# Odd experts' results copied by VectorE instead of ScalarE, in both experts' stages

## The reference, cut to what matters

```
x = x + 0.5 * ffn(layernorm(x));  x = x + attn(layernorm(x));  x = x + 0.5 * ffn(layernorm(x))

def ffn(h):                       # 64 experts, 2 per token, at most 256 rows each
    x = rmsnorm(h) * rms_w
    probs = softmax(x @ gate_w.T);  topk_w, topk_ids = top_k(probs, 2), weights normalised
    xb = rows of x sorted into 64 experts x 256 slots
    g, u = split(xb @ w13)        # 256 -> 2 x 128, for each expert
    yb = (silu(g) * u) @ w2       # 128 -> 256, for each expert
    out = sum over the 2 experts of topk_w * yb[slot]
    return out + silu(x @ sw_gate) * (x @ sw_up) @ sw_down + h
```

## Time and profile before

| | us |
|---|---|
| median of 3 runs | 2152.15 (2151.78 to 2154.71) |
| profiled execution | 2146.13 |
| its span, first to last instruction | 2144.4 |
| PE busy | 1966.8 (92%) |
| DVE busy | 1317.7 (61%) |
| ACT busy | 1083.9 (51%) |
| POOL busy | 1115.9 (52%) |

### The profile page before, as it was taken

One profiled execution on the slowest core, in us unless ns is written; L12 is line 12 of the kernel. 1 busy time (PEld: TensorE's weight loads), 2 busy tenths in 40 slices (PEclk: granted clock), 3 DMA queues, 4 the chain that ended last, 5 costly groups with the idle time before them and its releaser, 6 DMA issues.

```text
span 2144.4 us, 32641 instructions
## 1 busy us (share of the span) xinstructions
PE 1966.8 (92%) x11134; PEld 1673.0 (78%) x11134; DVE 1317.7 (61%) x3471; ACT 1083.9 (51%) x1989; POOL 1115.9 (52%) x1251
## 2 busy tenths in 40 slices
PE   6996899599999999999999999999999974898887
PEld 4665888578888888888888888888888864788754
DVE  5996666455566566576576575575575453555477
ACT  6873666344445455454454454454454432555653
POOL 6775677344254555546545645645535326666500
PEclk9998999899999999999999999999999987999999
DMA  9434899790022032022121110110100203988678
GB/s 280 151 128 145 273 294 301 249 302 21 1 99 79 21 98 80 21 99 64 36 95 37 67 47 23 49 40 21 60 11 21 89 13 85 300 285 304 228 247 275
DMA packets 236407, 270.09 MB, mean 126 GB/s; under 512 B 25489, under 2 KB 186322, under 8 KB 236242
## 3 DMA queue, kind: packets, MB, share of 16 engines
q1 hardware_dynamic: 199122, 192.40, 27.8%
q0 software_dynamic: 28672, 67.22, 9.5%
q10 hardware_dynamic: 8448, 8.39, 1.2%
HBM read 150.35 MB, written 117.57 MB: 125 GB/s over the span
## 4 chain that ended last, share of the span: by engine, by line
PE 64%; DVE 6%; issue 4%; ACT 4%; POOL 2%; DMA 1%; another core or an unknown queue 1%; ACTq 0%; DVEq 0%; SPq 0%; POOLq 0%
PE attention_ring L1961 21%; PE attention_acc L1991 14%; PE attention_acc L1981 8%; PE attention_acc L2181 2%; DVE attention_hid_l L1687 2%; PE attention_work L2054 2%; PE attention_ring L2207 2%; PE attention_work L2070 2%; PE attention_work L2074 2%; PE attention_work L2037 2%; PE attention_ring L2171 2%; PE attention_acc L2171 1%; ACT final_xf L1443 1%; PE attention_work L1949 1%; PE attention_work L2011 1%
## 5 line engine op out<-in xcount | busy, mean ns | idle before, releaser
L1687 DVE TENSOR_TENSOR attention_hid_l<-attention_gelu,attention_hid_h 128x512 fp32r<-128x512 f32 x384 | 285.2, 743 | 470.7 <-ACT attention_gelu L1327 284.4
L1324 ACT ACTIVATE attention_hid_h<-attention_ring,home_b 128x512 fp32r<-128x512 f32 x384 | 264.2, 688 | 539.3 <-PE attention_ring L1961 468.4
L1327 ACT ACTIVATE attention_gelu<-attention_ring,home_b 128x512 f32<-128x512 f32 x384 | 261.6, 681 | 0.0
L1961 PE MATMUL attention_ring<-attention_n_t_h,home_w_h 128*128 128x512 f32 x512 | 203.9, 398 | 1.6 <-DVE attention_n_t_l L1679 1.6
L1991 PE MATMUL attention_acc<-attention_hid_h,home_w_h 128*128 128x512 f32 x512 | 201.1, 393 | 2.8 <-DVE home_room L1704 1.3
L1961 PE MATMUL attention_ring<-attention_n_t_h,home_w_l 128*128 128x512 f32 x512 | 199.9, 390 | 0.0
L1991 PE MATMUL attention_acc<-attention_hid_l,home_w_h 128*128 128x512 f32 x512 | 199.6, 390 | 0.0
L1961 PE MATMUL attention_ring<-attention_n_t_l,home_w_h 128*128 128x512 f32 x512 | 199.5, 390 | 0.0
L1991 PE MATMUL attention_acc<-attention_hid_h,home_w_l 128*128 128x512 f32 x512 | 199.3, 389 | 0.0
L1166 POOL DMA_INDIRECT home_room<-expert_rows,routing_slots x128 | 135.7, 1060 | 93.2 <-issue 53.3
L1302 POOL DMA_INDIRECT token_rows<-home_room,attention_gelu x128 | 128.6, 1005 | 90.8 <-ACT home_room L1423 43.2
(11 more groups left out here) (298 smaller groups left out, 5250.1 us busy)
## 6 DMA issues: line engine op xcount, KB each, us to landing
experts_w<-in_L_ffn_w SPq DMA_DIRECT2D x64, 256.0 KB
expert_rows<-experts_y SPq DMA_DIRECT2D x64, 256.0 KB
slot_rows<-const_zeros SPq DMA_DIRECT2D x16, 1024.0 KB
token_rows<-const_zeros SPq DMA_DIRECT2D x16, 1024.0 KB
home_room<-in_L_ffn_w SPq DMA_DIRECT2D x64, 256.0 KB
home_room<-slot_rows SPq DMA_DIRECT2D x64, 256.0 KB
final_y_rows<-token_rows SPq DMA_DIRECT2D x32, 512.0 KB, 7.8
dispatch_x_in<-in_L_attn_x SPq DMA_DIRECT2D x16, 512.0 KB, 6.3
```

The lines of the kernel that those rows point to most:

```text
L1324: act.activation(hid[n % PARTS][0][:, :], ring[n % RING][:, :], ACT.Gelu, bias=b1[:, m, c:c + 1])
L1327: act.activation(gelu[n % GELUS][:, :], ring[n % RING][:, :], ACT.Gelu, bias=b1[:, m, c:c + 1]).then_inc(ring_free, 1)
L1687: dve.tensor_tensor(hid[n % PARTS][1][:, :], gelu[n % GELUS][:, :], hid[n % PARTS][0][:, :].bitcast(fp32), ALU.subtract).then_inc(hid_read ...
L1961: last = pe.matmul(ring[n % RING][:, :], w1[m][wp][:, k, c * P:(c + 1) * P], rows_t[xp][:, k, :], start=(q == 0), stop=(q == 2 * len(TERMS ...
```

## The change

In both experts' stages the copies of the results of odd experts move from ScalarE (`activation` with Copy) to VectorE (`tensor_copy`, a COPY in the profile). Pass e of the loop now has `copy_y(e-1)` on ScalarE if e is odd and on VectorE if e is even, there between `split_rows(e+3)` and `gated(e+1)`. The copy of expert 63 is VectorE's, behind its loop. The semaphore becomes two, one for each parity: `down(e)` waits for the one of its own parity. The same edits in the first stage (`experts`) and in the second (`attention_to_end`); of the pairs one is shown.

```diff
-        y_ready, y_copied = sem("y_ready"), sem("y_copied")
+        y_ready, y_copied = sem("y_ready"), [sem("even_y_copied"), sem("odd_y_copied")]
...
             def store(e):
-                sp.wait_ge(y_copied, e + 1)
+                sp.wait_ge(y_copied[e % 2], e // 2 + 1)
...
@@ scalar @@
-                act.activation(y[e % R][:, :, :], ps_y[e % F][:, :, :], ACT.Copy).then_inc(y_copied, 1)
+                act.activation(y[e % R][:, :, :], ps_y[e % F][:, :, :], ACT.Copy).then_inc(y_copied[0], 1)
...
                     round_rows(e + 3)
-                if e:
+                if e and e % 2:
                     copy_y(e - 1)
                 if e + 1 < EXPERTS:
                     gate(e + 1)
...
-            copy_y(EXPERTS - 1)
...
@@ vector @@
+            def copy_y(e):
+                dve.wait_ge(y_ready, e + 1)
+                if e >= R:
+                    dve.wait_ge(y_stored[e % R], 16 * (e // R))
+                dve.tensor_copy(y[e % R][:, :, :], ps_y[e % F][:, :, :]).then_inc(y_copied[1], 1)
...
                     split_rows(e + 3)
+                if e and e % 2 == 0:
+                    copy_y(e - 1)
                 if e + 1 < EXPERTS:
                     gated(e + 1)
...
+            copy_y(EXPERTS - 1)
...
@@ tensor @@
                 if e >= F:
-                    pe.wait_ge(y_copied, e - F + 1)
+                    pe.wait_ge(y_copied[e % 2], e // 2)
...
@@ second stage, gpsimd @@
             for e in range(EXPERTS):
-                pool.wait_ge(y_copied, e + 1)
+                pool.wait_ge(y_copied[e % 2], e // 2 + 1)
...
@@ second stage, tensor, behind the loop @@
-            pe.wait_ge(y_copied, EXPERTS)
+            for done in y_copied:
+                pe.wait_ge(done, EXPERTS // 2)
```

More of the change, by code:

```diff
@@ L1015, in attention_to_end @@
         we_rounded, we_split, gate_up_ready, silu_ready = sem("we_rounded"), sem("we_split"), sem("gate_up_ready"), sem("silu_ready")
-        hidden_ready, y_ready, y_copied = sem("hidden_ready"), sem("y_ready"), sem("y_copied")
+        hidden_ready, y_ready, y_copied = sem("hidden_ready"), sem("y_ready"), [sem("even_y_copied"), sem("odd_y_copied", late=True)]
         sw_loaded, total_loaded = sem("sw_loaded"), [sem(f"total_loaded{s}") for s in range(FR)]
@@ L1422, in copy_y @@
                     act.wait_ge(y_stored[e % YR], 16 * CH * (e // YR))
-                act.activation(y[e % YR], ps_y[e % EF], ACT.Copy).then_inc(y_copied, 1)
+                act.activation(y[e % YR], ps_y[e % EF], ACT.Copy).then_inc(y_copied[0], 1)
             round_weights(0)
@@ L1465, in _ @@
                     round_rows(e + 3)
-                if e:
+                if e % 2:
                     copy_y(e - 1)
@@ L1868, in final_scales, with copy_y @@
                 dve.wait_ge(halved, 2)
+            def copy_y(e):
+                dve.wait_ge(y_ready, e + 1)
+                if e >= YR:
+                    dve.wait_ge(y_stored[e % YR], 16 * CH * (e // YR))
+                dve.tensor_copy(y[e % YR], ps_y[e % EF]).then_inc(y_copied[1], 1)
             out_scales(last)
@@ L2178, in expert_down @@
                 if e >= EF:
-                    pe.wait_ge(y_copied, e - EF + 1)
+                    pe.wait_ge(y_copied[e % 2], e // 2)
                 for c in range(CH):
```

## The result

| | median of 5 runs, us | lowest to highest |
|---|---|---|
| before | 2151.78 | 2148.91 to 2154.71 |
| changed | 2161.30 | 2160.69 to 2163.97 |

The ratio is 1.0048 with the interval 1.0028 to 1.0067, so the changed kernel is slower by 10.3 us (6.0 to 14.4). The forecast was +3.5 us.

The account below looks back on a forecast made before the run. TensorE was taken to set the pace in undisturbed steps, with its waits for hidden values deciding the cost; 3.6 + 0.4 - 0.5 = +3.5 us on 2152.15 gave 2155.7 us, range 2146.5 to 2162.

Parts of the forecast that it names:

- Undisturbed steps: Expert steps where TensorE sets the pace: VectorE's copy fits into its 0.70 us gap, cost 0.
- Steps with a slice: Six first-stage steps behind home's weight slices: the copy delays hidden values and matmul 0.60 us each, +3.6 us.
- Late steps: Second-stage steps with late ScalarE work: only even step 56 pays, 0.44 us; odd ones nothing; +0.4 us.
- rival B: Odd results hold up GpSimd's second-stage scatters and late steps change parity: +9.9 us, 2162.1 us; chance 0.14.
- End of the second stage: Expert 63's copy leaves ScalarE, whose chain into the last part starts 0.48 us earlier: -0.5 us.
- Added waits: VectorE's copy waiting for the result and the store of the expert four before: neither wait binds, 0.
- A: Rival: transfers pace both stages, so later late steps shrink by the stall; -0.5 to +0.5 us, 2152.2; chance 0.20.
- C: Rival: ScalarE's earlier silu is used in second-stage waits; -4.1 us taken, 2148.0, reaching to -7.7; chance 0.20.
- D: Rival: VectorE's copies hold up GpSimd's row gathers, 5.2 us; +8.7 us with the forecast, 2160.9; chance 0.04.

Follow-up runs that it names:

- f1: Whole change, but the six results copied in steps behind home's slices stay on ScalarE; -0.4 us (-2.1 to +1.5) against the kernel before.
- k1: Change in the first stage alone, repeated in the group where the kernel before takes 2159 us; +5.2 us (2.4 to 8.0) against it.
- g1: All copies on ScalarE, ScalarE made late in 15 even second-stage passes; +19.9 us (16.2 to 23.7) against the kernel before.
- g4: Hand-made lateness in 15 odd second-stage passes, that stage's odd results copied by VectorE; +18.5 us (15.1 to 21.6) against the kernel before.
- k2: Change in the second stage alone, in the group where the kernel before takes 2159 us; +2.2 us (-0.4 to +4.7) against it.
- c0: Control: all copies on ScalarE as in the kernel before, only the copy counting rewritten; -0.4 us (0.9998) against it, quick group.
- e2: Change in the second stage alone, in a quick group; -0.2 us (-2.3 to +1.9) against the kernel before.
- f3: Whole change with VectorE's copy behind the hidden values instead of ahead, both stages; +9.0 us (6.3 to 11.8) against the kernel before.
- g2: Hand-made lateness in 15 even second-stage passes, that stage's odd results copied by VectorE; +23.7 us (19.7 to 27.9) against the kernel before.
- g3: All copies on ScalarE, hand-made lateness in 15 odd second-stage passes; +19.5 us (15.7 to 23.3) against the kernel before.

## Why the prediction was wrong

**Undisturbed steps, 0: right**, in quick groups and in the others.

**Steps with a slice, +3.6 us: right in mechanism, and the term that was sized wrong.** In a quick group the six named steps carry the loss: f1 takes the six copies away and the loss is gone. They cost 3.3 us there by the waits, and the first stage +4.2 as timed. In the traces with late steps the six cost 11.6 and 12.9 us unchanged and 17.4 and 21.1 changed, a mean of 7.0 more and not 3.6. The step that failed is "The same 0.60 us, six times, is 3.6 us". The 0.60 us of each copy is there, 3.6 us. But the sum let every subtraction start where it had started before. It starts 0.32 us later on average, which is 1.9 us, and together that makes up the 5.6 us of the waits. The remaining 1.4 us lies in the steps but not in the waits, and the sum had no term for it: in k1 three steps with slower matmuls behind the wait lose 1.23 us more than the others each. Why the subtraction starts later stays open: the silu ahead of the rounding is seen later, as above, and I can't say why. These are two traces of each kind, and the timed +5.2 us of k1 (2.4 to 8.0) is nearer to the forecast.

**Late steps, +0.4 us: the price of one was right, the list was not.** g1 to g4 give 0.45 us in an even pass and 0 in an odd one, against 0.44 and 0. What was wrong is that I counted the late steps of the kernel before and kept their number, parity and length. The last table above shows what became of them. With the change the odd passes lose 24.0 and 19.6 us, and 9.5 to 11.6 without, although nothing was moved in these passes. In the changed trace the even passes lose 6.1 us where they lost 16.3, so there the loss has mostly moved from even to odd. From the sixth step on that trace loses 31.4 us, against 30.0 to 33.0 in the three unchanged ones, and what it has beyond the trace before lies in the first five steps, 8.5 us and not 3.5, where k1, unchanged, has 7.0. Only k2 loses more throughout, 39.4 us from the sixth step on. The timed second stage gives +2.2 us with 0 inside the interval. So it is shown that the late steps don't keep their parity, and not shown that the change makes the second stage's late steps cost more.

**The sum.** Timed alone, the first stage costs +5.2 us and the second +2.2. Of the 10.3 us 3 are not accounted for; the intervals are wide enough to take them. The measured 2161.3 us lies just below the upper end of the range, 2162; that end was there for rival B, which is not what happened.

**End of the second stage, -0.5 us: wrong, 0.** From the start of expert 62's gate and up matmuls to the end of the program it is 127.65 us in c0 and 127.64 in e2. ScalarE's silu and TensorE's transposes there, c0 and then e2:

```profile
1982.65 0.59 ACT L1476 ACTIVATE final_silu<-attention_ring 128x512 f32<-128x512 f32 x1
...
1985.39 1.04 PE L2230 MATMUL attention_work<-const_eye,final_xf 128*128 128x128 f32 x8
```

```profile
1978.17 0.60 ACT L1476 ACTIVATE final_silu<-attention_ring 128x512 f32<-128x512 f32 x1 [1.86 <-PE attention_ring L2239]
...
1982.27 1.04 PE L2230 MATMUL attention_work<-const_eye,final_xf 128*128 128x128 f32 x8
```

Expert 62's matmuls start at 1971.99 in c0 and 1968.88 in e2, so the silu starts 1.36 us earlier (10.66 and 9.30 behind them), but the transposes stay at 13.40 us behind them in both, and TensorE has no idle time ahead of them. They do not hang on the silu. The 2.01 us wait of the earlier trace rows is not there in these two traces, and its row names no engine that it waited for; I had taken it for a wait on ScalarE's scalings.

**Added waits, 0: right** as the kernel stands; f3 shows the bank's wait come into force as soon as the copy moves back by one place.

**Rivals.** A (transfers pace the stage) falls in the quick groups: the window of c0 moves 352 GB/s with TensorE without a gap, and 3.3 us of longer home steps were not given back. With late steps the timed +5.2 us of k1 speaks against it too, but the late steps' own cause is unknown. C (ScalarE's relief) has g2 against it, where the earlier silu is not used, and with whole slices no run with the change was faster beyond its interval. D falls with the gathers of 0.95 us beside copies in f3. By the rule of the Trainium skill ("SBUF — State Buffer", "Who interferes with whom") a VectorE instruction with at most one SBUF input, outside the double-rate modes, doesn't contend with GpSimd; the copy reads PSUM only, its 0.68 us show no double rate, and the trace agrees. B named nearly the number that came out, 2162.1, and that is luck. Late steps do change parity in the changed trace, but into odd passes, where B charges nothing; it needed them in even ones. And its other half, a scatter that starts late and delays the next late step, is not shown: GpSimd waits 4.0 us more (40.1 and 36.1), and g4, with the odd results copied late and lateness added, costs nothing more than g3.

Open is what the late steps are, why they move under the change, and what makes a group quick. One idea, that TensorE's results are seen late while GpSimd issues indirect DMAs back to back, has the quick groups against it: in c0 GpSimd issues nearly all of them 0.30 us apart and nothing is late. Removing the gathers or scatters where there are late steps was not tried.

## What to carry to other kernels

Before work is moved to an engine with room on average, look for the few steps in which its queue is full ahead of something that the pacing engine waits for: in the quick groups 6 of 64 moved copies made the cost, and exchanging even and odd avoided it. A long piece in such a queue (2.3 us in a 2.77 us step) is better cut in two, which won 4.4 us there, as much as the change had lost, and 5.6 us in the group with late steps. The wait behind such a piece is where the piece starts plus what stands behind it, and both belong into the sum. And stalls without a cause in the trace should not be carried over as a fixed list: their number and place are part of the unknown, and the range should say so.

## What the runs showed of the hardware

The same kernel takes about 2100 us in some groups of runs and 2152 to 2159 us in others, and chip 13 of the record is in one of each. The traces before and c0 differ by 44.8 us, 43.3 of them in the steps of the two experts' stages: from expert 62 of the first stage to the first transpose of the second it is 1408.9 us in the trace before and 1409.2 in c0. Where they differ, ScalarE stands idle ahead of instructions that wait for TensorE (1.79 us in the pass shown), while ScalarE's copy of 128x512 takes 0.59 us at the median in both.

Behind waits of TensorE of the same length, 2.69 us, the granted clock was 1.00 once and 0.50 (1.2 GHz) another time, and the four second matmuls took 1.13 and 2.08 us.

A copy of 128x512 from PSUM takes 0.68 us on VectorE and 0.60 from start to start, as x_lo does, and does not stretch a gather of GpSimd (0.95 us beside it), which a subtraction of two SBUF tiles does (3.00 us beside the slice, at 290.76 in the changed trace).
